# Inverting the softmax totals on 128x16 between two block transposes, and the cosine product of K in PSUM

## The reference, cut to what matters

```
q = rope(layernorm(x) @ Wq)      # 32 heads of 128
k = rope(ctx @ Wk); v = ctx @ Wv # 8 KV heads, 4 query heads share one
logits  = 30 * tanh(q k^T * 0.0884 / 30), masked
weights = softmax(logits)
x = x + tanh(g_xattn) * (weights @ v) @ Wo
x = x + tanh(g_ffn) * ffn(layernorm(x))   # ffn: 4-bit weights, silu(x Wg) * (x Wu) @ Wd
rope(t) = t * cos + rotate_half(t) * sin
```

## Time and profile before

| what | value |
|---|---|
| median of 3 runs | 858.85 us (857.18 to 859.26) |
| profiled execution, span from first to last instruction | 856.9 us |
| runs above that span | 0.3 us (lowest) to 2.4 us (highest); the median is 1.95 us above |
| TensorE busy | 800.7 us, 93% |
| VectorE busy | 777.9 us, 91% |
| GpSimd busy | 521.8 us, 61% |
| ScalarE busy | 360.0 us, 42% |
| mean granted TensorE clock | 0.986 |
| VectorE's reciprocal, L933 | 64 of 3346 ns, 214.1 us |

### The profile page before, as it was taken

One profiled execution on the slowest core, in us unless ns is written; L12 is line 12 of the kernel. 1 busy time (PEld: TensorE's weight loads), 2 busy tenths in 40 slices (PEclk: granted clock), 3 DMA queues, 4 the chain that ended last, 5 costly groups with the idle time before them and its releaser, 6 DMA issues. The chain is left out here.

```text
span 856.9 us, 12479 instructions
## 1 busy us (share of the span) xinstructions
PE 800.7 (93%) x3937; PEld 654.0 (76%) x3937; DVE 777.9 (91%) x1115; ACT 360.0 (42%) x722; POOL 521.8 (61%) x391
## 2 busy tenths in 40 slices
PE   5789999999999999999999999999888779898998
PEld 4677888888878888888878888888776556676786
DVE  7899999999998999999999999999998989898631
ACT  3655444443444344434443444334443434444420
POOL 3679765666557656665666566668885466666500
PEclk9999999999999999999999999999999889999999
DMA  8220302010110201021020102010200234331011
GB/s 297 79 75 12 111 2 74 1 50 17 58 52 1 74 1 50 1 74 49 0 73 0 49 0 73 3 33 0 50 6 1 54 77 85 77 83 43 1 61 37
DMA packets 56085, 40.36 MB, mean 47 GB/s; under 512 B 23436, under 2 KB 43404, under 8 KB 56044
## 3 DMA queue, kind: packets, MB, share of 16 engines
q1 hardware_dynamic: 56044, 39.81, 16.0%
HBM read 37.70 MB, written 2.10 MB: 46 GB/s over the span
## 5 line engine op out<-in xcount | busy, mean ns | idle before, releaser
L933 DVE RECIPROCAL r_tot<-ps_tot 128x512 f32<-128x512 f32 x64 | 214.1, 3346 | 0.0
L501 POOL TENSOR_TENSOR aT_lo<-attn,aT_hi 128x512 fp32r<-128x512 f32 x64 | 87.5, 1367 | 172.0 <-ACT aT_hi L668 171.9
L628 ACT CAST qT_hi<-ps_qT 128x512 fp32r<-128x512 f32 x64 | 37.5, 586 | 180.8 <-PE bank_kv L1112 96.3
L51 PE MATMUL bank_q<-wq_hi,xT_hi 128*128 128x512 f32 x256 | 107.1, 418 | 1.2 <-DVE wq_lo L796 1.2
L51 PE MATMUL ps_o<-wo_hi,aT_hi 128*128 128x512 f32 x256 | 101.2, 395 | 1.8 <-POOL aT_lo L501 1.1
L53 PE MATMUL bank_q<-wq_hi,xT_lo 128*128 128x512 f32 x256 | 101.9, 398 | 0.0
L52 PE MATMUL bank_q<-wq_lo,xT_hi 128*128 128x512 f32 x256 | 101.8, 398 | 0.0
L53 PE MATMUL ps_o<-wo_hi,aT_lo 128*128 128x512 f32 x256 | 100.2, 391 | 0.0
L52 PE MATMUL ps_o<-wo_lo,aT_hi 128*128 128x512 f32 x256 | 100.1, 391 | 0.0
L486 POOL TENSOR_TENSOR probs<-probs,keepT 128x512 f32<-128x512 f32 x64 | 85.3, 1333 | 1.3 <-ACT probs L644 1.3
L514 POOL TENSOR_TENSOR roped<-q_cos,q_sin 128x512 f32<-128x512 f32 x61 | 79.1, 1296 | 10.7 <-DVE q_sin L817 10.7
(11 more groups left out here) (228 smaller groups left out, 2223.7 us busy)
## 6 DMA issues: line engine op xcount, KB each, us to landing
wo_raw<-in_Wo SPq DMA_DIRECT2D x8, 1024.0 KB, 5.2
wq_raw<-in_Wq SPq DMA_DIRECT2D x7, 1024.0 KB, 5.7
packed<-in_gate_q SPq DMA_DIRECT2D x40, 64.0 KB, 2.3
packed<-in_up_q SPq DMA_DIRECT2D x40, 64.0 KB, 2.3
packed<-in_down_q SPq DMA_DIRECT2D x10, 256.0 KB, 3.4
acc<-in_x SPq DMA_DIRECT2D x8, 256.0 KB, 8.1
wkv_raw<-in_Wk SPq DMA_DIRECT2D x8, 256.0 KB, 5.9
wkv_raw<-in_Wv SPq DMA_DIRECT2D x8, 256.0 KB, 6.4
```

The lines of the kernel that those rows point to most:

```text
L51: nc.tensor.matmul(out, w_hi, m_hi, start=first, stop=False)
L501: nc.gpsimd.tensor_tensor(aT_lo[:], attn[:], aT_hi[:].bitcast(F32), ALU.subtract).then_inc(a_split, 1)
L933: nc.vector.reciprocal(r_tot[:], ps_tot[:]).then_inc(inverted, 1)
```

## The change

The reciprocal over 128x512 is replaced by three instructions. The first transposes the totals in blocks of 32x32 from PSUM into `r_tot`. Since all rows of the totals are alike, column 0 of each transposed block holds the 32 totals of that block, one on each partition. The second takes the reciprocal of those 16 columns (128x16, every 32nd element of `r_tot`) into the new tile `r_small`. The third transposes `r_small`, each column repeated 32 times, back into `r_tot`, which then holds the 512 reciprocals on every partition as before. Two more semaphores, `tot_turned` and `r_spread`, order the three and the multiply behind them.

The product `k * cos` goes to block 3 of the slot's own PSUM bank instead of the SBUF tile `k_cos`, which is gone; the sum into `roped` reads it there.

```diff
-        k_cos = sb("k_cos", [P, D], F32)
+        r_small = sb("r_small", [P, GC // 32], F32)
...
-                        rope_products(kv_bank(s)[:, 0:1, :], k_cos[:].unsqueeze(1), k_sin[:].unsqueeze(1), cs_tab, k_mul)
+                        rope_products(kv_bank(s)[:, 0:1, :], kv_bank(s)[:, 3:4, :], k_sin[:].unsqueeze(1), cs_tab, k_mul)
                         wait(dve, k_mul, j + 1)
                         wait(dve, tr_done, j)
-                        nc.vector.tensor_tensor(roped[:, HG, :], k_cos[:], k_sin[:], ALU.add).then_inc(k_roped, 1)
+                        nc.vector.tensor_tensor(roped[:, HG, :], kv_bank(s)[:, 3, :], k_sin[:], ALU.add).then_inc(k_roped, 1)
...
                         wait(dve, tot_done, j - 1)
                         wait(dve, norm_done, j - 2)
-                        nc.vector.reciprocal(r_tot[:], ps_tot[:]).then_inc(inverted, 1)
+                        nc.vector.transpose(r_tot[:], ps_tot[:]).then_inc(tot_turned, 1)
+                        wait(dve, tot_turned, j - 1)
+                        nc.vector.reciprocal(r_small[:], r_tot[:].rearrange("p (c e) -> p c e", e=32)[:, :, 0]).then_inc(inverted, 1)
                         wait(dve, inverted, j - 1)
+                        nc.vector.transpose(r_tot[:].rearrange("p (c e) -> p c e", e=32),
+                                            r_small[:].unsqueeze(2).to_broadcast([P, GC // 32, 32])).then_inc(r_spread, 1)
+                        wait(dve, r_spread, j - 1)
                         wait(dve, pv_done, j - 1)
                         wait(dve, a_split, j - 2)
                         nc.vector.tensor_tensor(attn[:], ps_pv[:], r_tot[:], ALU.mult).then_inc(norm_done, 1)
```

More of the change, by code:

```diff
@@ L235, in flamingo_block @@
         tot_done, inverted, norm_done = sem("tot_done"), sem("inverted"), sem("norm_done")
+        tot_turned, r_spread = sem("tot_turned"), sem("r_spread")
         a_rounded, a_split, o_done, acc_done = sem("a_rounded"), sem("a_split"), sem("o_done"), sem("acc_done")
```

## The result

The median fell from 858.85 us (3 runs; a fourth, of 992.96 us, was disturbed and is not counted) to 835.98 us (4 runs, 835.38 to 836.25). The ratio is 0.9735, 95% interval 0.9721 to 0.975. The forecast was 836.5 us. A second measurement of the same changed kernel on another chip gave 836.43 us and again 0.9735 (0.9716 to 0.9753). The profiled span went from 856.9 to 833.4 us: 23.5 us less, where the prediction's sum was 22.3.

The account below looks back on a forecast made before the run. TensorE's 9.34 us floor per slot was taken as the bound, VectorE exceeding it in some. Middle 8.9, opening 4.5, last slots 5.5 and handover 3.4 sum to 22.3 us, giving 836.5 us; own range 833 to 840.

Parts of the forecast that it names:

- The bound: Attention slots: TensorE's floor is 9.34 us; VectorE sets the pace only in some slots, by about 0.47 us each.
- the four slots of 8.41 us: Four slots from 262.46 to 299.80 us, 9.34 us each, TensorE without a gap, VectorE busy only 8.41 per slot.
- the slower rival: Slow 32-bit transposes: at 2.56 us each the chain is 5.5 us, +42 us, 901 us; chance 0.06.
- The chain's price: Two transposes of 0.69 us, a 0.25 us reciprocal and waits: 1.75 us per slot in place of 3.38.
- The second transpose held by GpSimd: Rival: it waits up to 1.3 us for GpSimd's mask; gain 17 us, time 841.5 us; chance 0.15.
- The sum into `roped`: Per slot on VectorE: one SBUF source fewer saves 0.68 us on average, 1.02 in a slot of 9.8.
- Middle: Slots 6 to 56: the 8.9 us that slots of 9.8 take over TensorE's floor all go.
- the stall by issue of 1.5 us: One step in slots 6 to 56: stall counted with its tail as 1.7 us of surplus, left where it is.
- Opening: First steps of 14.58, 13.41 and 10.51 us: 4.5 of 7.0 us surplus won, then GpSimd's own work sets the step.
- Last eight slots: Slots from 566.68 to 637.09 us: `kT_lo` comes 2.1 us earlier, winning 5.5 of 6.2 us.
- Handover: Passage from attention to feed-forward block: wait for `attn` falls from 2.40 to 0.76 us, `p_lo` becomes last; 3.4 us won.
- another 1.6: Handover: the next totals, behind a second reciprocal, come another 1.6 us earlier.

Follow-up runs that it names:

- the moved parts: Changed kernel with head 1's weight split on GpSimd (and its rounding on ScalarE) moved to later opening steps: 833.22 us, ratio 0.971.

## Why the prediction was right, point by point

**The bound.** Right, and shown from both sides: 9.34 us is TensorE's floor. Neither the chain left out (some 1.75 us less of VectorE's work per slot) nor 1.48 us more of it moves a typical slot, and one matmul less moves it by 0.20 us. Where VectorE would take over again was put too high, 4.8 us of chain against some 3.9 measured. The prediction took 0.5 us off the four slots of 8.41 us for the shorter sum, but in those slots the sum already took 0.29 us (see the middle, below): VectorE is busy 27.66 / 4 = 6.92 us there now, where 6.3 was forecast. The price of the slower rival has a slip too: its 42 us stand over TensorE's floor, so they belong on top of some 836.5 us and give 878, not 901.

**The chain's price.** 0.707 + 0.254 + 0.711 and three waits of 0.03 to 0.04, 1.78 us against 1.75. The line through a 128x1 instruction and the full reciprocal gave 248 ns for the small one; it takes 254. A transpose was taken at 0.69 us, by the row of `attn`; it takes 0.71. The estimate made from a figure of the Trainium skill (VectorE: DVE Perf Modes, "The three transpose paths") was 0.71 us, and the trace agrees with it.

**The second transpose held by GpSimd.** It was not. In the slot of the changed kernel below, GpSimd's mask runs from 305.91 to 307.21 and the transpose inside it. The sum into `roped` (304.95) likewise runs inside GpSimd's own sum (304.30 to 305.59) and is not held:

```profile
304.30 1.29 POOL L515 TENSOR_TENSOR roped<-q_cos,q_sin 128x512 f32<-128x512 f32 x1
...
304.95 0.29 DVE L922 TENSOR_TENSOR roped<-bank_kv,k_sin 128x128 f32<-128x128 f32 x1
305.16 0.71 DVE L934 STREAM_TRANSPOSE r_tot<-ps_tot 128x512 f32<-128x512 f32 x1
305.90 0.25 DVE L936 RECIPROCAL r_small<-r_tot 128x16 f32<-128x16 f32 x1
305.91 1.30 POOL L487 TENSOR_TENSOR probs<-probs,keepT 128x512 f32<-128x512 f32 x1 [0.32 <-ACT probs L645]
306.19 0.71 DVE L938 STREAM_TRANSPOSE r_tot<-r_small 128x512 f32<-128x512 f32 x1
```

All 64 lie between 711 and 712 ns.

**The sum into `roped`.** 291 ns against 277 expected. What the prediction had not counted is `p_lo`: its mean fell from 1181 to 753 ns, since VectorE now reaches it before GpSimd has begun `aT_lo`, which is longer instead (1367 to 1513 ns on average). That is 23 us more of VectorE's time. Either part alone brings it; what it is worth by itself no run shows.

**Middle.** 8.9 us predicted for the slots of 9.8, and 10.25 won. The difference is the stall by issue of 1.5 us, counted with its tail as 1.7 us that stay. In no other version profiled was a stall by issue at the transposes of Q longer than 0.36 us, those with the old chain among them, so it looks like a matter of that one execution; what made it stays open. But the trace speaks against its being a cost of its own. These are rows of the kernel before:

```profile
246.08 1.22 DVE L903 TENSOR_TENSOR p_lo<-probs,p_hi 128x512 fp32r<-128x512 f32 x1
...
253.10 0.63 PE L1111 MATMUL ps_qT<-ident,roped 128*128 128x128 f32 x4 [1.55 <-issue]
...
255.54 0.68 DVE L903 TENSOR_TENSOR p_lo<-probs,p_hi 128x512 fp32r<-128x512 f32 x1
...
287.18 0.29 DVE L921 TENSOR_TENSOR roped<-k_cos,k_sin 128x128 f32<-128x128 f32 x1
287.26 1.37 POOL L514 TENSOR_TENSOR roped<-q_cos,q_sin 128x512 f32<-128x512 f32 x1
...
302.70 1.55 DVE L903 TENSOR_TENSOR p_lo<-probs,p_hi 128x512 fp32r<-128x512 f32 x1
```

While TensorE stood still VectorE caught up. For the next slots it reached `p_lo` and the sum into `roped` before GpSimd had begun its own instruction, and they took 0.68 and 0.29 us with the same operands as before; then it fell behind and they were long again. The ten slots behind the stall (253.10 to 346.50) take 9.34 us each. In the kernel before with one matmul less, where no such stall occurs, the ten slots at the same place take 9.60 each, and slots 6 to 56 take 487.34 us, no less than the 486.94 with the stall. So, as far as two executions can show it, the stall was paid back while VectorE set the pace, and all of the 10.6 us over TensorE's floor were VectorE's. The four slots on which the prediction read that floor were slots behind the stall; the floor was right all the same.

**Opening.** 4.5 against 5.2 us. Of the latter 0.8 is before step 2, where the versions differ by more than that (step 2 begins between 39.6 and 41.6 us), 2.5 in step 2 and 1.9 in step 3. The limit that the prediction named was right: GpSimd held step 3, as the moved parts showed. In step 2 the granted clock was 0.88 before, so part of it ran at 1.2 GHz, and 1.00 after. With the product alone it was 1.00 too, and the step took 13.67 us (columns as in the earlier trace rows):

```profile
39.62:53.29 13.67, 10.83 (x58) 8.48 (x58) 13.53 (x18) 7.00 (x15) 9.99 (x10) 1.00 0.28 98
```

So 1.6 us of this step are the chain's at an equal clock; the 0.9 us between 14.58 and 13.67 can be the product's, the clock's or both. Its new length is not explained: 12.1 us in all eight versions with the PSUM product and a chain no longer than the new one, the one without a chain (12.09) among them. TensorE waits there 0.70 us for `kT_lo` and 0.52 for GpSimd's sum, and no run took either apart.

**Last eight slots.** 5.5 predicted, 5.5 measured.

**Handover.** This is the term that was mis-sized: 3.4 predicted, 1.9 won. Its first half came: the wait for `attn` fell from 2.40 to 0.81 us (predicted 0.76), and the first totals start 4.95 us after the stretch begins instead of 6.59. The "another 1.6" of the second reciprocal did not. From these totals to the next, TensorE needs 6.17 us instead of 6.28 (before, then changed):

```profile
643.68:649.96 6.28, 6.21 (x21) 4.67 (x22) 6.18 (x8) 1.74 (x4) 3.31 (x4) 0.73 0.00 0
```

```profile
621.11:627.28 6.17, 4.89 (x22) 3.61 (x22) 5.85 (x11) 2.10 (x4) 5.00 (x5) 1.00 0.00 0
```

Before, TensorE was busy nearly throughout, partly at 1.2 GHz (granted clock 0.73), so it hardly waited for that reciprocal. Now the clock is 1.00, as the prediction thought it might be, but TensorE waits: not for `p_lo`, which the prediction had put last, but 1.05 us for `aT_lo`, behind the mask on GpSimd. In all, the next totals start 11.12 us after the stretch begins instead of 12.87, which is 1.75 us and not 3.4. The size is also uncertain by the one profile of the kernel before: two other versions with the old chain took 33.27 and 33.31 us for the handover, not 32.46.

**The forecast's sizes against each other.** The errors (+0.7, +1.35, 0, -1.5, +0.7) partly cancel: the time was hit to 0.5 us, while single terms were off by up to 1.5. The mechanism was right; so close a hit was luck.

## What to carry to other kernels

When two engines are level, the worth of a cut is what one of them exceeds the other's floor by, not what is cut: here 158 us of VectorE's time bought 23.5, and the tile moved to PSUM, which took 58 us off VectorE by itself, bought 13. A stall of the engine that is not the bound need not be a term of its own: the other engine may use it to catch up. Look for a slot in which the suspected engine happens to be partly idle; its length is the floor, and the gain is the distance of the other slots from it. After such a change a small edit on the other engine can pay that was worth nothing before (here 12.7 us): try again what had failed.

## What the runs showed of the hardware

A block transpose of 128x512 in 32 bits takes 0.707 us from PSUM and 0.711 from SBUF with a broadcast input, about the 0.69 us of `attn`, a plain 128x512 instruction; GpSimd's mask did not hold it. By its two sizes a reciprocal costs VectorE 6.2 ns an element of each partition: (3346 - 254) / (512 - 16) = 6.23. And one SBUF operand fewer in a sum that runs beside GpSimd was worth 667 ns of its mean (958 to 291), more than twice what the sum itself takes. What it saves is the wait for GpSimd's instruction: with both operands in SBUF the sum took 1.30 us when it started 0.13 us behind GpSimd's, and 0.29 when it started 0.08 us ahead of it.
